# Two superblocks in one pass over the node blocks: a gated graph network on one Trainium2 core

## What is computed

```python
h = relu(layernorm(x)) @ lin_w.T + lin_b
for i in range(3):
    m = h @ weight[i]
    agg = segment_sum(m[src], dst, num_segments=n_nodes)
    gi = agg @ w_ih.T + b_ih ; gh = h @ w_hh.T + b_hh
    r = sigmoid(ir + hr) ; z = sigmoid(iz + hz)
    n = tanh(inn + r * hn)
    h = (1.0 - z) * n + z * h
out = x + h
```

## Time and profile before

| | us |
|---|---|
| median of 3 runs | 3904.65 (3902.16 to 3905.36) |
| the profiled execution | 3896.86 |
| its span in the profile | 3895.0 |
| granted TensorE clock, mean | 0.952 of full speed |

### The profile page before, as it was taken

The page is one execution under the profiler, slowest core; times in us unless marked ns, Lnnn a source line. Parts: engine busy times, 40 slices in busy tenths (PEclk is TensorE's granted clock), DMA queues, the critical chain, the costliest instruction groups (busy, mean ns, idle before and its releaser), DMA issues.

```text
span 3895.0 us, 74412 instructions
## 1 busy us (share of the span) xinstructions
PE 3452.6 (89%) x25008; PEld 2729.5 (70%) x25009; DVE 2870.7 (74%) x8189; ACT 3020.0 (78%) x4231; POOL 2756.7 (71%) x2758
## 2 busy tenths in 40 slices
PE   6289999999979999987999999999979999999996
PEld 4167666766667777765777777777757777777775
DVE  7478888888867777765777777777757777777774
ACT  4179888888878888776788788787857887878783
POOL 4777777777777777733777777777737777777776
PEclk8699999999989999998999999999989999999998
DMA  8346566565577666665666666666756666666664
GB/s 274 108 152 216 187 197 208 185 200 196 180 240 235 192 198 198 191 183 169 194 204 199 198 202 207 192 205 191 227 159 191 205 197 196 204 194 202 194 201 121
DMA packets 461502, 758.66 MB, mean 195 GB/s; under 512 B 66760, under 2 KB 337864, under 8 KB 461128
## 3 DMA queue, kind: packets, MB, share of 16 engines
q1 hardware_dynamic: 216472, 411.54, 33.0%
q0 software_dynamic: 129408, 265.20, 24.6%
q10 hardware_dynamic: 115248, 77.10, 6.4%
HBM read 578.11 MB, written 175.47 MB: 193 GB/s over the span
## 4 chain that ended last, share of the span: by engine, by line
PE 43%; POOL 23%; DVE 11%; issue 10%; ACT 7%; DMA 4%; DVEq 2%; ACTq 0%; SPq 0%; POOLq 0%
POOL ring_region L565 23%; PE psum L860 18%; PE psum L842 16%; ACT wide_counts L682 4%; DVE quad_onehots L1249 2%; PE psum L815 2%; PE psum L827 2%; DMA states<-temps 2%; DVE aggT L1188 2%; DVEq L1140 2%; DVE message_halves L1285 1%; PE psum L785 1%; PE psum L786 1%; PE psum L787 1%; ACT quad_counts L709 1%
## 5 line engine op out<-in xcount | busy, mean ns | idle before, releaser
L565 POOL DMA_INDIRECT ring_region<-messages,edge_src x2696 | 2702.7, 1002 | 1048.7 <-issue 804.2
L860 PE MATMUL psum<-wide_counts,message_halves 128*128 128x504 f32 x8036 | 1988.3, 404 | 149.7 <-DVE message_halves L1285 129.7
L682 ACT CAST wide_counts<-messages_region 128x1008 fp32r<-128x1008 uint8 x1722 | 1880.7, 1170 | 257.9 <-PE psum L860 202.6
L860 PEld LDWEIGHTS psum<-wide_counts,message_halves 128*128 128x128 f32 x8036 | 1517.0, 192 | 516.5 <-ACT wide_counts L682 111.9
L1285 DVE TENSOR_TENSOR message_halves<-messages_region,message_halves 128x256 fp32r<-128x256 f32 x1722 | 810.9, 471 | 59.3
L842 PE MATMUL psum<-quad_onehots,block_onehots 128*128 128x238 bf16 (+2 forms) x6272 | 768.3, 272 | 60.6 <-ACT quad_counts L709 42.4
L709 ACT CAST quad_counts<-psum 128x504 uint8<-128x504 f32 x1568 | 770.6, 643 | 28.5 <-PE psum L842 26.5
L842 PEld LDWEIGHTS psum<-quad_onehots,block_onehots 128*128 128x128 bf16 x6272 | 539.7, 100 | 276.4 <-issue 47.6
L1283 DVE CAST message_halves<-messages_region 128x256 fp32r<-128x256 f32 x1722 | 656.7, 381 | 64.0 <-PE psum L860 35.2
L1249 DVE TENSOR_SCALAR quad_onehots<-iota_quad,count_keys 128x1666 bf16<-128x1666 f16 (+2 forms) x896 | 528.3, 652 | 0.0
L827 PEld LDWEIGHTS psum<-onehot,ring_region 128*128 128x128 bf16 x8088 | 243.4, 96 | 187.2 <-issue 160.3
(11 more groups left out here) (104 smaller groups left out, 1529.3 us busy)
## 6 DMA issues: line engine op xcount, KB each, us to landing
messages_region<-counts SPq DMA_DIRECT2D x574, 441.0 KB
counts<-quad_counts SPq DMA_DIRECT2D x224, 441.0 KB
ring_region<-messages,edge_src POOLq DMA_INDIRECT x2696
messages<-pieces_out ACTq DMA_DIRECT2D x98, 192.0 KB
messages_region<-plain SPq DMA_DIRECT2D x21, 896.0 KB, 7.6
temps<-states ACTq DMA_DIRECT2D x98, 128.0 KB
states<-temps ACTq DMA_DIRECT2D x98, 128.0 KB
plain<-temps ACTq DMA_DIRECT2D x98, 128.0 KB
```

Source lines behind the costliest of these rows:

```text
L565: nc.gpsimd.indirect_dma_start(out=rows[:, n % RING, h * QC + c, :], out_offset=None, in_=messages[layer], in_offset=bass.IndirectOffsetOn ...
L682: nc.scalar.copy(wide_counts[:, v % UBUF, :, cols], stage[v % ABUF][:, :, cols]).then_inc(s_wide, 1)
L860: mm = nc.tensor.matmul(psum[:, 6 + kg % 2, 0:DQ * W], halves[:, v % UBUF, b % HB, half * P:(half + 1) * P], wide_counts[:, v % UBUF, :, c ...
```

## The change

- A pass over the 98 blocks takes two superblocks (`TOGETHER`): for each block and half PE issues one matmul for each of the two, with the same half of the messages, into two PSUM banks. Two pairs of banks take turns: 6 and 7, 4 and 5. Layer 0 has 9 superblocks, so its last pass has one. There are 21 passes.
- What was a unit is now an item of a pass: one split, but two widenings. Halves are buffered for 6 items, wide counts for 3.
- Banks 4 and 5 being taken, the gathered sums after step 91 use bank 1 alone, and `rows_ready` waits for the adds of the step before instead of those of two steps before.
- The sums of both superblocks of a pass are added at its end, 28 windows in a row. A tile waits for the pass, so tiles come five to seven in a row, then none for six steps. The last tile of layers 1 and 2 is at step 98.
- 4 count buffers instead of 3.

```diff
-ABUF = 3
+ABUF = 4
+TOGETHER = 2
+DENSE_BANKS = ((6, 7), (4, 5))
...
         begun = DENSE_FROM[layer] + i * GSB
-        dense = begun + GSB - 1 - (LEAD if layer else 0)
+        passed = PASS_MEMBERS[PASS_OF[DENSE0[layer] + i]][-1] - DENSE0[layer] + 1
+        dense = DENSE_FROM[layer] + passed * GSB - 1 - (LEAD if layer else 0)
...
+                room += STEP_UNITS
+                begun = x
+                while x < max(begun, end) and room >= len(PASS_MEMBERS[ITEMS[x][0]]):
+                    room -= len(PASS_MEMBERS[ITEMS[x][0]])
+                    x += 1
...
         def window(n, q):
-            return psum[:, 4 + n % 2, q * W:(q + 1) * W]
+            if n < TURN:
+                return psum[:, 4 + n % 2, q * W:(q + 1) * W]
+            return psum[:, 1, q * W:(q + 1) * W]
...
                 if v >= ABUF:
-                    sp.wait_ge(s_wide, UN * (v - ABUF + 1))
+                    sp.wait_ge(s_wide, LOAD_WIDENED[v - ABUF])
...
             def rows_ready(n):
                 pe.wait_ge(s_oh, n + 1)
-                if n >= 2:
+                if n > TURN:
+                    pe.wait_ge(s_add, 2 * n)
+                elif n >= 2:
                     pe.wait_ge(s_add, 2 * (n - 1))
...
+            def dense_item(x):
+                p, j, unit, v = ITEMS[x]
+                members = PASS_MEMBERS[p]
...
+                for b in range(*UNITS[unit]):
+                    cols = slice(b * W, (b + 1) * W)
+                    for half in range(HALVES):
+                        for a in range(len(members)):
+                            mm = nc.tensor.matmul(
+                                dense_bank(p, a), halves[:, x // UN % UBUF, b, half * P:(half + 1) * P],
+                                wide_counts[:, (v + a) % UBUF, :, cols], start=(j == 0 and b == 0 and half == 0),
+                                stop=(j == SLICES - 1 and b == HB - 1 and half == HALVES - 1))
...
             def add_superblock(layer, kg, s):
-                dve.wait_ge(s_dense, UN * SLICES * (kg + 1))
+                k, p = superblock_of(kg), PASS_OF[kg]
+                dve.wait_ge(s_dense, PASS_ITEM[p + 1])
...
-                    ended = [kg for kg, where in summed.items() if where == (layer, s)]
-                    for w in units.get((layer, s), ()):
-                        while ended and UN * SLICES * (ended[0] + 1) <= w - UBUF * UN:
+                    ended = [kg for p, where in summed.items() if where == (layer, s) for kg in PASS_MEMBERS[p]]
+                    for x in splits.get((layer, s), ()):
+                        while ended and PASS_ITEM[PASS_OF[ended[0]] + 1] <= split_over(x):
                             add_superblock(layer, ended.pop(0), s)
-                        split(w)
+                        split(x)
                     for kg in ended:
                         add_superblock(layer, kg, s)
```

213 lines of the change are left out of this document (115 added, 98 removed).

## The result

The changed kernel takes 4059.24 us (median of 4 runs, 4057.28 to 4063.37) against 3903.4 for the kernel before: a ratio of 1.0406, 95% interval 1.0392 to 1.0421. The prediction said slower and was right in that, but 3969 us is 90 us too low, and the measured time lies above the range. The profiled execution has a span of 4055.5 us.

A forecast was written before the change was run, and what follows sets the result against it. PE was taken to set the pace in layers 0 and 1, POOL in layer 2. Terms 2 − 5 + 5 + 22 + 26 + 3 + 11 = +64 us on 3896.9, plus 7.8 for the median, gave 3969 us; range 3885 to 4020.

The forecast's parts named there:

- The one bank: Ends of passes: next gathered sums wait for 28 adds and those of the gathered windows; PE idles 9.0 us each.
- ACT in bursts: Tiles in a row make ACT late by 0 to 11 us a burst; taken as 5 in layer 1, 3.5 in layer 0.
- rival (a): ACT is the bound in bursts, 9 to 11 us late in each; 4015 us, chance 0.15.
- (b): Rival: ACT's lead is enough, so the terms for bursts fall away; 3895 us, chance 0.13.
- Layer 1: Steps 784.7, tiles 137.3, ends 96, bursts 40: 1058.0 us against 1035.6, +22.
- Layer 0: Dense stage: ends 39.6 and ACT's bursts 17.5, sum 57 for 62 us, −5; its start +2.
- Border 1 to 2: More dense matmuls and three more tiles between layer 1's last gathered sums and layer 2's first gather: +26 us.
- Border 0 to 1: Last pass has one superblock, 2.6 us shorter; step 150 puts matmuls and widenings before the last tile's stores, +8; in all +5.
- Layer 2: PE takes 989 us for 986.4, slightly over POOL's 977: +3.
- Tail: Last tile is two steps later, at 5.4 us a step: +11 us.
- (c): Rival: the second matmul of a pair is cheaper, since it uses the same half of the messages; 3894 us, chance 0.07.
- (d): Rival: ends cost little, with register loads running beside the adds; 3845 us, chance 0.15.

The follow-up runs named there:

- e4: Changed kernel with up to three widenings of a step put ahead of ACT's middle piece, which waits for DVE; 3964.3 us, 1.0160 of the kernel before.
- the controls: Kernel before with one bank for gathered windows from step 91 (0.9992), adds in two parts of seven (1.0027), or four count buffers (0.9984).
- e12: Changed kernel with no dense matmuls of layer 2 issued before that layer's first gathered sums; 4071.2 us, 1.0431 of the kernel before.
- e1: Changed kernel with the 14 adds of a pass's second superblock made one step later on DVE; 3969.9 us, 1.0167 of the kernel before.
- e3: Changed kernel with second superblock's adds a step later and tiles every second step; 3925.5 us, 1.0052 of the kernel before.
- e2: Changed kernel with tiles every second step inside a layer instead of five to seven in a row; 3948.8 us, 1.0117 of the kernel before.

## Why the prediction was wrong in size

**The one bank: right.** Forecast 9.0 at each end and 72 us in layer 1, measured 75.0. Idle of this kind had not existed before, and "PE asks 7.3 us after the end" held. In layer 0 the wait stands at the gate products, as said, at three of the four ends: 21.3 us, 7.1 each, for 6.8. At the fourth the same adds show as a wait for halves:

```profile
1695.66 2.02 PE L908 MATMUL psum<-wide_counts,message_halves 128*128 128x504 f32 x4 [10.47 <-DVE message_halves L1331]
```

DVE makes its 28 adds from 1680.5 to 1693.5 us, and the split comes behind them. That makes 31.8 us in layer 0 for 27.2. In layer 2 it is 68.1 us for 72, but partly by luck: seven waits of 7.1 on average, one of 16.0 at the last end, where PE has no dense matmuls left to run, and three of 0.75 behind it.

**ACT in bursts: the mechanism right, the size too small. This is the step that failed.** It reads "Late by 0 to 11 us a burst; I take 5 in layer 1 and 3.5 in layer 0, the middle", 57.5 us in all. Taking the wait away (e4) showed 60.8 / 8 = 7.6 in layer 1 and 33.2 / 5 = 6.6 in layer 0, 94.0 us, so 36 us more. The idle itself was sized nearly right: 64.1 of the 94.0 are idle of PE that went (42.4 in layer 1, 21.7 in layer 0). The other 29.9 are slow matmuls, which the term had at nothing. The forecast costed the clock at ends of passes alone, and the granted clock fell behind ACT's lateness as well. The lateness had been seen in one row of layer 0 (3.27, in the second tile of three, with the store that DVE waited for ahead of it); layer 1 of before has 46 such waits, 2.0 us on average and up to 8.2. The 7.6 lies between the 5 of the forecast and the 9 to 11 of rival (a), which had a chance of 0.15; the lead that (b) counted on did not suffice.

**Layer 1** by the forecast's own terms: 784.7 + 137.3 for steps and tiles, 75.0 for the adds (72), 47.9 for widened counts, 10.1 for the ring (0), together 1055.0. The remaining 35.8 us are slow matmuls; e4 took 18.4 of them with ACT's waits, which leaves 17.4 for the ends (24). So of the 33 us that were missing, 26 are ACT's bursts (47.9 + 18.4 for 40), 10 the ring and 3 the adds, and the slow matmuls at ends give 7 back. The ring's waits had been there before, 7.5 us in layer 1, and "What is left is 62 us over 8 ends of superblocks and 105.5 over 16" spread them over the ends; the sum of after then had no term for them. Of the 105.5, 58.0 were waits for halves, 3.6 an end, and some 39 slow matmuls.

**Layer 0: wrong by 20**, of which ACT's bursts make 15.7 (33.2 for 17.5) and the adds 4.6; what is left nearly cancels. The +2 for the start of the dense stage was measured as +7.2, but 4.1 of these had come by step 91, where both kernels still build the counts and nothing of the change runs. The kernels before of the controls reach step 91 at 1137.4 to 1140.5 us, with 1135.1 before and 1139.2 after. From there to the dense stage it takes 32.3 us for 29.3: +3.0.

**Borders: right in kind, small in size.** Border 1 to 2: 64.5 to the first gather for 53. To the end of the last gate products it takes 46.8 us where it took 14.4, 32.4 more for the 26 forecast; PE's waits for widened counts (5.3 us) and slow matmuls behind them had no term. The rest fails in "The 20 matmuls after the last gate products lie beside DVE's and ACT's work": from there to the first gather it takes 17.7 us for 12.6, and 13.2 in e12, where these matmuls and their widenings are gone. Border 0 to 1: +17.0 for +5. Its term for step 150 was +8; from the last gate products, at 1809.6, to the first gather, at 1846.0, it takes 36.4 us, where it took 23.0 before: +13.4.

**Layer 2: wrong by 12, and near only by luck.** POOL's share came: the indirect DMA went from 990 to 974 ns (forecast 968), its own time from 993.9 to 977.6 us (977), and in e1 to e3 the layer settles at 974 to 976, 12 us under before.

```profile
L608 POOL DMA_INDIRECT ring_region<-messages,edge_src x768 | 748.2, 974 | 356.8 <-issue 229.4 <-DMA messages<-pieces_out 96.6 <-PE psum L874 30.8
```

The 30.8 us are what went wrong: from the fourth end of a pass on, POOL waited around each end for PE, which stood there, to free the ring. It had no such wait in this layer before, and has none in e1 to e3. The forecast took PE as the bound instead, with "918.6 of its own". That counts 140 dense matmuls (2856 in this stage after, 2996 before; 33.5 us by 0.239) that now run ahead of layer 2; without them its sum is 956, and POOL's 977 is the bound. Two errors made the +3.

PE's waits for widened counts are 27.7 us in layer 2, for 16. No middle piece is made there, and e4 left them alone; e2, with tiles spread, took them away. ACT's 78.9 us ahead of widenings that end with DVE's last step of a tile are the likely place. The Trainium skill's page "SBUF — State Buffer", section "Who interferes with whom", says that an instruction of DVE with two SBUF inputs contends with one of GpSimd that reads SBUF; the 974 ns agree, with DVE's two-input splits halved.

**Tail: +13.5 for +11.** Tiles follow each other by 4.26 us, from ACT's first gate of one to that of the next, less than the 5.4 I took, but three of them are added rather than two (four stand behind the last gathered sums, where one did):

```profile
4038.89 0.47 ACT L670 ACTIVATE temps<-psum,small 128x256 f32<-128x256 f32 x1 [2.17 <-PE psum L858]
...
4043.15 0.47 ACT L670 ACTIVATE temps<-psum,small 128x256 f32<-128x256 f32 x1 [2.17 <-PE psum L858]
```

**Rivals.** (c) fell: 28 matmuls take 6.72 us, 0.24 each, with the same half in both of a pair, and there are still 25009 loads for 25008 matmuls. Weights that are loaded once for many matmuls, of which the Trainium skill's page "TensorE: Matmul & The Clock Gate", section "Step-by-step: what each phase is for", speaks, no run here shows. (d) fell: between each seven adds DVE idles 1.60 to 1.68 us for the register loads, which do not run beside them.

## What to carry to other kernels

Lay a residue of a stage's time against the list of waits of that stage before dividing it by the number of events one has in mind, and look where each wait lies: here 17.7 us of a list belonged to the stage before, 7.5 to another cause than the ends, and only 58.0 of 105.5 to the wait that the residue was put down to. When work is made in bursts, cost what a wait leaves behind it as well as the wait: in the granted clock it was worth half as much again here (29.9 us for 64.1). Ask on each engine what stands behind the instruction that waits. ACT's timeline shows its widenings in the program's order behind the piece that waits for DVE; putting three of them, which need nothing of it, ahead was worth 95 us, though the wait itself was hardly longer than before the change (93.2 us for 90.1 in layer 1). And ask which engine paces each stage after the change: a term for one that does not is worth nothing. Halving the work of an engine that is not the bound buys little, and what is grouped to do it (sums added late, tiles given late, a layer's end pushed back) is paid at the borders: repaired as far as I could, the change gains 54 us inside the stages and loses over 70 outside them.

## What the runs showed that I had not expected

The idle at pass ends and the clock are not tied as I had thought. In e1_defer 63 us of idle in eight waits went from layer 1 and the time fell by no more than the idle that went, 51 us in all; the slow matmuls stayed. In e4_widen_first 42 us went in 16 short waits of up to 5.9, and 18 us of slow matmuls with them. The record of the granted clock shows where. In layer 1 of the changed kernel it is at the lower level in 17 stretches: one at each of the 8 ends, 7 in the bursts, each after a wait of 4.4 to 5.9 us for widened counts, and 2 at the layer's start. In e4 the 7 are gone. In e1 the long ones at the ends are gone, but seven short ones are new (three of them near ends), after waits of 1.6 to 2.6 us. Of the time at the lower level PE spent 73.5 us outside idle after, 65.5 in e1 and 40.5 in e4; the rest it stood still, and there a low clock costs nothing.

One bank of PSUM for windows that PE writes and DVE reads in turn, which looks like the risk of such a change, cost nothing measurable (0.9992) as long as DVE's other work in a row stayed at 7.2 us.
